# Mamba prologue: which weights the first group of loads holds, and when the convolution's diagonals are made

## What is computed

```python
xz = einsum('bld,ed->ble', hidden_states, in_proj_w)        # hidden_states: layer norm of x, 16 x 512 x 256
x, z = xz[..., :d_inner], xz[..., d_inner:]                 # d_inner = 512
xc = depthwise_conv(x, conv_w, width 4, causal) + conv_b
u = xc * sigmoid(xc)
x_dbl = einsum('bld,ed->ble', u, x_proj_w)                  # dt_lo, B_ssm, C_ssm
delta = softplus(dt_lo @ dt_proj_w.T + dt_proj_b)
A = -exp(A_log)
h = exp(delta * A) * h + (delta * u) * B_t                  # over the 512 steps
y = (h . C_t) + u * D_param
out = (y * silu(z)) @ out_proj_w.T
```

## Time and profile before

| | us |
|---|---|
| median of 3 runs | 3397.47 |
| lowest and highest of them | 3393.35, 3407.66 |
| the profiled execution | 3421.41 |
| its span in the profile | 3419.6 |

### The profile page before, as it was taken

One profiled execution on the slowest core, in us unless ns is written; L12 is line 12 of the kernel. 1 busy time (PEld: TensorE's weight loads), 2 busy tenths in 40 slices (PEclk: granted clock), 3 DMA queues, 4 the chain that ended last, 5 costly groups with the idle time before them and its releaser, 6 DMA issues.

```text
span 3419.6 us, 54089 instructions
## 1 busy us (share of the span) xinstructions
PE 2720.6 (80%) x20202; PEld 1499.2 (44%) x20202; DVE 2304.3 (67%) x2483; ACT 1717.5 (50%) x3115; POOL 2152.2 (63%) x1317
## 2 busy tenths in 40 slices
PE   5778778887788877888652699977888888359998
PEld 2333333343334433343332455555665666235665
DVE  1799999999999999999985322115556555542211
ACT  3677777777777777777640222223333433122222
POOL 1899999999999999999970344433333333024542
PEclk9899999988899998999775799989999999679999
DMA  3456555666556665565522133330111111213432
GB/s 110 106 134 154 142 136 128 146 147 147 131 135 139 149 143 137 139 141 131 142 63 59 40 78 82 88 60 26 39 51 39 45 39 39 65 31 82 87 88 25
DMA packets 227391, 330.01 MB, mean 97 GB/s; under 512 B 40545, under 2 KB 116833, under 8 KB 227010
## 3 DMA queue, kind: packets, MB, share of 16 engines
q1 hardware_dynamic: 202562, 292.49, 34.5%
q0 software_dynamic: 24576, 34.10, 5.9%
HBM read 240.52 MB, written 85.98 MB: 95 GB/s over the span
## 4 chain that ended last, share of the span: by engine, by line
PE 41%; DVE 24%; POOL 21%; issue 8%; ACT 3%; DMA 1%; another core or an unknown queue 1%; SPq 0%; DVEq 0%; POOLq 0%; ACTq 0%
POOL m_side L584 13%; DVE m_pair L668 8%; POOL m_hc L593 7%; PE f_h L1341 7%; PE g_h L1341 6%; PE t_wb L2056 6%; DVE m_hc L668 5%; PE f_yp L1355 3%; PE m_wk L771 3%; PE g_yp L1355 3%; DVE m_hc L677 2%; PE t_num L2056 2%; PE m_y L863 2%; PE m_pair L919 2%; PE t_a_ps L2056 2%
## 5 line engine op out<-in xcount | busy, mean ns | idle before, releaser
L584 POOL TENSOR_TENSOR m_side<-m_du_r,m_bc 128x1024 f32<-128x1024 f32 x416 | 974.8, 2367 | 13.6 <-DMA m_du_r<-ddd 13.3
L351 ACT ACTIVATE m_pair<-m_delta_r,m_a_neg 128x512 f32<-128x512 f32 x832 | 539.7, 681 | 179.3 <-DVE m_hc L677 128.8
L593 POOL TENSOR_TENSOR m_hc<-m_hc,m_bc 128x1024 f32<-128x1024 f32 x208 | 492.2, 2369 | 96.5 <-DVE m_hc L668 94.7
L668 DVE TENSOR_TENSOR_SCAN m_pair<-m_pair,m_side 128x1024 f32<-128x1024 f32 x240 | 548.0, 2284 | 3.3 <-ACT m_pair L351 2.8
L863 PE MATMUL m_y<-m_hc,m_fold 128*32 128x512 f32 x2048 | 321.6, 702 | 229.8 <-DVE m_hc L677 121.1
L668 DVE TENSOR_TENSOR_SCAN m_hc<-m_pair,m_side 128x1024 f32<-128x1024 f32 x176 | 397.9, 2276 | 25.9 <-ACT m_pair L351 25.9
L677 DVE TENSOR_TENSOR m_hc<-m_pair,m_bc 128x1024 f32<-128x1024 f32 x304 | 370.7, 1219 | 7.3
L771 PE MATMUL m_wk<-m_xnT,m_w_in 128*128 128x512 f32 x512 | 273.9, 662 | 11.2 <-DVE m_cw_diag L725 10.3
L771 PE MATMUL m_wk<-m_xs,m_cw_diag 128*128 128x512 f32 x512 | 246.1, 609 | 15.5 <-ACT m_xs L416 15.5
L919 PE MATMUL m_pair<-m_b_diag,m_du_t 128*32 128x128 f32 x6144 | 203.7, 289 | 43.6 <-DVE m_hc L668 24.4
L919 PEld LDWEIGHTS m_pair<-m_b_diag,m_du_t 128*32 128x32 f32 x6144 | 178.8, 117 | 124.9 <-issue 123.5
(11 more groups left out here) (308 smaller groups left out, 4929.9 us busy)
## 6 DMA issues: line engine op xcount, KB each, us to landing
m_delta_r<-ddd SPq DMA_DIRECT2D x256, 256.0 KB, 6.8
m_du_r<-ddd SPq DMA_DIRECT2D x256, 256.0 KB, 7.7
m_bc<-bcd SPq DMA_DIRECT2D x256, 128.0 KB, 2.9
ddd<-m_delta SPq DMA_DIRECT2D x32, 512.0 KB, 3.5
ddd<-m_du SPq DMA_DIRECT2D x32, 512.0 KB, 4.2
f_w<-in_w SPq DMA_DIRECT2D x24, 512.0 KB
g_w<-in_w SPq DMA_DIRECT2D x24, 512.0 KB
m_xt<-in_x SPq DMA_DIRECT2D x16, 512.0 KB, 10.8
```

The costliest lines, as they stand in the source:

```text
L351: last = nc.scalar.activation(to, delta_r[:, c % 2, q, :], ACT.Exp, scale=a_neg[:, c * NQ + q, st:st + 1])
L584: nc.gpsimd.tensor_tensor(side[:, un % RING, :, :], du_r[:, c % 2, 2 * h:2 * h + 2, :], bc[:, 0, st:st + 1, :].to_broadcast([P, 2, T]), AL ...
L593: nc.gpsimd.tensor_tensor(hc[:, un % RING, :, :], hc[:, un % RING, :, :], bc[:, 1, st:st + 1, :].to_broadcast([P, 2, T]), ALU.mult).then_i ...
L668: nc.vector.tensor_tensor_scan(to, decay, added, 0.0, ALU.mult, ALU.add).then_inc(S["scan"], 1)
```

## The change

Four things. `m_conv_w` and `m_conv_b` are counted with the first group of loads (they are still issued third and fourth of the weights, at the same place in SP's order). DVE waits for the first group and makes the convolution's diagonals first, raising `diag` once for each channel tile; only then does it wait for the second group, make `m_d_diag` (with a new semaphore `ddiag`) and negate `m_a_neg`. PE no longer waits for `diag` ahead of `ix`, but for `dt + 1` of it ahead of each `conv`, and waits for `ddiag` ahead of `xp`. ACT waits for the first group ahead of its loop over `dt`, and takes the exponential of `A_log` behind the second `cv_out`, with the wait for the second group there.

```diff
-        first_loads = [(ident, w["ident"]), (w_in, w["in_T"])]
-        loads = [(conv_w, w["conv_w"]), (conv_b, w["conv_b"]), (a_log, w["a_rep"]),
-                 (w_x, w["x_T"]), (w_dt, w["dt_T"]), (d_par, w["d_par"]),
+        first_loads = [(ident, w["ident"]), (w_in, w["in_T"]), (conv_w, w["conv_w"]), (conv_b, w["conv_b"])]
+        loads = [(a_log, w["a_rep"]), (w_x, w["x_T"]), (w_dt, w["dt_T"]), (d_par, w["d_par"]),
                  (w_out, w["out_T"]), (w_g, w["g_P"]), (fold, w["fold"])]
...
-                act.wait_ge(S["ld_w"], 16 * len(loads))
-                nc.scalar.activation(a_neg[:], a_log[:], ACT.Exp).then_inc(S["a_exp"], 1)
+                act.wait_ge(S["ld_w0"], 16 * len(first_loads))
                 for dt in range(KD):
                     ix_out(0, dt)
                     cv_out(0, 0, dt)
+                    if dt == 1:
+                        act.wait_ge(S["ld_w"], 16 * len(loads))
+                        nc.scalar.activation(a_neg[:], a_log[:], ACT.Exp).then_inc(S["a_exp"], 1)
...
-                dve.wait_ge(S["ld_w"], 16 * len(loads))
-                dve.wait_ge(S["a_exp"], 1)
-                nc.vector.tensor_scalar(a_neg[:], a_neg[:], LEAST, -1.0, ALU.max, ALU.mult).then_inc(S["aneg"], 1)
                 dve.wait_ge(S["ld_w0"], 16 * len(first_loads))
-                for k in range(KD):
-                    nc.vector.tensor_scalar(d_diag[:, k, :], ident[:], d_par[:, k:k + 1], None, ALU.mult)
                 for k in range(KD):
                     for i in range(CW):
                         last = nc.vector.tensor_scalar(cw_diag[:, k, i, :], ident[:], conv_w[:, k, i:i + 1], None,
                                                        ALU.mult)
-                last.then_inc(S["diag"], 1)
+                    last.then_inc(S["diag"], 1)
+                dve.wait_ge(S["ld_w"], 16 * len(loads))
+                for k in range(KD):
+                    last = nc.vector.tensor_scalar(d_diag[:, k, :], ident[:], d_par[:, k:k + 1], None, ALU.mult)
+                last.then_inc(S["ddiag"], 1)
+                dve.wait_ge(S["a_exp"], 1)
+                nc.vector.tensor_scalar(a_neg[:], a_neg[:], LEAST, -1.0, ALU.max, ALU.mult).then_inc(S["aneg"], 1)
...
-                pe.wait_ge(S["diag"], 1)
                 for dt in range(KD):
                     ix(0, dt)
+                    wait_alone(pe, S["diag"], dt + 1, S["tick"])
                     conv(0, dt, 0)
                     conv(0, dt, 1)
                 pe.wait_ge(S["ld_w"], 16 * len(loads))
                 pe.wait_ge(S["one"], 1)
+                pe.wait_ge(S["ddiag"], 1)
```

More of the change, by code:

```diff
@@ L183, in mamba @@
         wk = s.ps("wk", [P, 2, T])
-        first_loads = [(ident, w["ident"]), (w_in, w["in_T"])]
-        loads = [(conv_w, w["conv_w"]), (conv_b, w["conv_b"]), (a_log, w["a_rep"]),
-                 (w_x, w["x_T"]), (w_dt, w["dt_T"]), (d_par, w["d_par"]),
+        first_loads = [(ident, w["ident"]), (w_in, w["in_T"]), (conv_w, w["conv_w"]), (conv_b, w["conv_b"])]
+        loads = [(a_log, w["a_rep"]), (w_x, w["x_T"]), (w_dt, w["dt_T"]), (d_par, w["d_par"]),
                  (w_out, w["out_T"]), (w_g, w["g_P"]), (fold, w["fold"])]
         names = ("tick ld_w0 ld_w ld_x ld_xr st_x1 st_xn1 st_sc st_bc ld_bc0 ld_bc1 ld_bc2 ld_bc3 st_dd0 st_dd1 ld_r0 ld_r1 ld_r2 ld_r3 "
-                 "a_exp aneg const one halo diag "
+                 "a_exp aneg const one halo diag ddiag "
                  "bs agg ve rstd nm xn tr trev ix ixev cv cvev u iz izev sz xp xdev dt "
```

## The result

| | us | runs |
|---|---|---|
| before, median | 3401.94 | 21 |
| changed kernel, median | 3392.75 | 21 |
| ratio, with its 95% interval | 0.9976 (0.9969 to 0.9983) | |

The change saves 9.2 us by the medians and 8.2 us (5.8 to 10.5) by the ratio. The forecast was 9.6 us less, and the time 3387.9 in a range of 3377 to 3400. The median lies 4.9 above 3387.9; 4.5 of that is the kernel before, whose median was 3397.47 over three runs and is 3401.94 over 21.

A forecast was written before the change was run, and what follows sets the result against it. The prediction took the prologue's wait for the last weight (`m_fold`, landed at 19.06) as the bound: 9.6 + 0 + 0 − 0 = 9.6 us, so 3397.47 − 9.6 = 3387.9 us, range 3377 to 3400.

The forecast's parts named there:

- The wait that goes: PE's first projection waits only for `m_xnT` and starts at 14.07 instead of 23.66 us: gain 9.6 us.
- When the first group lands: Loads ahead of transposes and diagonals: landing taken as 10.3 us, between 9.8 and 19.06; costs 0 up to 11.30.
- The diagonals, the exponential, the added waits at cost 0: DVE's diagonals, ACT's exponential near 31 us and the new waits on DVE and PE are all covered: cost 0.
- The clock, a term of 0: TensorE's clock in the first channel tile and `xp`: same loss as before, 0; ends +5.5 and −6.1 us.
- The path: From the first projection the prologue is one PE-ACT chain to POOL's first scan input, which comes near 81 us.
- Rival A: TensorE's clock in the prologue comes back too: 5.5 us more gain, 3382.4 us; chance 0.12.
- Rival B: The first group's small loads land late, after 11.30 us: worst case gain 2.0 us, 3395.5 us; chance 0.06.
- Rival C: Something that doesn't move, a transfer above all, sets the first scan: no gain, 3397.5 us; chance 0.04.
- Rival D: TensorE's clock in the attention falls to 0.90, costing about 44 us: slower, 3431.9 us; chance 0.06.
- Carrying microseconds over: The prologue runs once, so the 9.6 us come off the median of the runs as microseconds, not as a share.

The follow-up runs named there:

- e1: The changed kernel without an edit, run once more as reference: 3390.21 us, ratio 0.9967 to the kernel before.
- e2: The changed kernel, but PE waits for all four channel tiles of diagonals ahead of its first projection: 3393.52 us, ratio 0.9972.
- e3: The changed kernel, but ACT takes the exponential, with its wait for the last weight, ahead of its loop again: 3393.33 us, ratio 0.9973.
- e5: The changed kernel, but PE's transposes wait for the last weight as well: 3398.08 us, ratio 0.9992.
- e7: The changed kernel with seven filler products of a zeroed tile on PE ahead of the first transpose: 3390.78 us, ratio 0.9977.
- e10: The changed kernel with filler products at four places on PE and half the `b_diag` tiles left to batch 0's first scan steps: 3396.86 us, ratio 0.9949.
- e12: The kernel before, unchanged, run once more: 3412.8 us, ratio 0.9994.
- e8: The changed kernel with PE fillers: seven ahead of the first transpose, four ahead of `xp`, eleven ahead of batch 1's transposes: 3389.87 us, ratio 0.9973.
- e4: The changed kernel, but the convolution's weights count with the second group again, and DVE and ACT wait for it: 3393.45 us, ratio 0.9974.
- e11: The kernel before, with the load of `m_w_dt` (97 partitions) cut into 96 and 1: 3407.26 us, ratio 0.9985.
- e6: The changed kernel with fills of six unread tiles on DVE delaying the layer norm, some 21 us of work: 3408.06 us, ratio 1.0025.

## Why the prediction was right

- **The wait that goes.** Right in place and size. Predicted start of the first projection 14.07, measured 14.10 in `e1` and `e2`; gain of this term 9.56, against 9.6.
- **When the first group lands.** I took 10.3; DVE starts on the diagonals at 9.49 in `e1`, and at 7.9 to 9.1 in `e2`, `e3`, `e5` and `e7` to `e10`. The lower end of 9.8, "`m_w_in`'s landing", was no bound: that transfer took 8.0 us in the profile of before, 6.5 in `e12` and between 5.4 and 5.8 in all others. It cost nothing, as a landing up to 11.30 is covered. The landing at 11.8, estimated with the fixed 2 us of the Trainium skill ("DMA: Bandwidth & Descriptors", Anatomy of one DMA, which gives it for transfers that GpSimd issues, while these are SP's), didn't come. `m_conv_b` landed 0.8 (`e8`) to 2.2 us (`e1`) behind `m_w_in`, so in `e1` the 2 us are about right, but `m_w_in` itself was there earlier.
- **The diagonals, the exponential, the added waits at cost 0.** Right. The exponential runs at 28.78 (not near 31, since the first channel tile was 2.2 us shorter), and delays nothing: the next copy starts 1.72 us after the start of the `cv_out` before it, as in the tiles beside it. The gap between a projection and its convolution is still 0.68 in all but the first tile. `e2`, `e3` and `e4` show besides that none of the three parts that they take back is worth more than about 1.4 us of waiting once the others are in, which the prediction had not said.
- **The clock, a term of 0.** The reason given beside it holds: the moment at which the clock rises isn't tied to the program (the rule of the Trainium skill, "TensorE: Matmul & The Clock Gate", Part 1; `e12` agrees, 7.97 against 10.03 us). That the term came out near 0 is luck. What I had missed are two more places, `dtp` and `iz`; the latter takes from 7.22 to 10.20 us. Between `before` and `e1` the first scan moved by 9.56 (first projection) + 2.22 (first channel tile) − 1.00 (`xp` and `dtp`) − 2.50 (`iz`) = 8.28 us, and for `e2` by 5.76.
- **The path.** Right up to POOL's input, but that input isn't what the first scan waits for. It waits for ACT in both kernels, whose work behind `iz` (9.44 us of `b_diag` tiles and more) the prediction doesn't name. The shift passes through it all the same.
- **Rival A** (all comes back) didn't happen by itself; `e10` shows its price when it is brought about. **Rival B**: `e5` gives its worst case at 21.72, as worked out, but the first group isn't late. **Rival C** (hidden anyway) falls by the table of scans (beyond some 3 us). **Rival D** (slower in the attention) isn't seen: the granted clock between 2400 and 2900 us is 0.98 in `e1`, where the last of the earlier trace rows has 0.99:

```profile
2400.00:2900.00 500.00, 435.14 (x4469) 311.38 (x4468) 292.36 (x477) 190.00 (x375) 179.60 (x182) 0.98 0.13 42
```

- **Carrying microseconds over.** Right: 8.2 (5.8 to 10.5) measured, 9.6 forecast.

## What to carry to other kernels

Where several loads count on one semaphore, ask for each waiter which of them it reads; the wait for the rest is pure loss, but only as long as nothing else covers it, so look for what is late next and stop where the parts are covered. Before a late load is worked around, look at why it is late: here one tile of 97 partitions held back all behind it. In a stretch that runs once, compare a landmark at its end (the first scan), not spans, which the later stages blur by more than such a change is worth.

## What the runs showed of the hardware

**A load of 97 partitions.** The first row is the transfer rate in the profile of before, in 40 slices from 12 to 20 us. The tail at 18 to 26 GB/s begins near 17.4 us; before it other transfers run beside it, so that the mean between 14 and 19 us is 130, not some 20 as the expectation of `e11` has it. In the second row, 17 to 19 us, the last two numbers are the mean busy share of the 16 transfer engines and GB/s: 0.07 is about one engine of sixteen (0.0625).

```profile
GB/s 98 169 164 143 232 312 379 364 287 271 169 72 87 143 205 230 215 205 379 353 348 220 189 149 47 31 41 20 20 20 23 18 26 20 26 26 26 20 26 26
...
17.00:19.00 2.00, 0.00 (x0) 0.00 (x0) 0.00 (x0) 0.00 (x0) 0.00 (x0) 1.00 0.07 25
```

With `m_w_dt` in 96 + 1 rows that tail is gone (`e11`). The Trainium skill ("DMA: Bandwidth & Descriptors", Why a DMA increments its semaphore by 16 and not by 1) says that a transfer uses the greatest number of engines, up to 16, that divides its outer size: worked out from that, one for 97 partitions and sixteen for 96. The 0.07 of the row and the missing tail in `e11` agree.

**The clock falls without a long wait.** I had looked for falls only in PE's long idle gaps, like the 4.20 us ahead of `xp`. In `e1` it fell once more between two halves of `dtp`, where PE was idle for 1.88 us (53.10 to 54.98), and in `e7` after 2.13 us. Busy time by stretch; the third number from the end is the granted clock:

```profile
54.00:55.00 1.00, 0.02 (x1) 0.02 (x1) 0.69 (x1) 0.97 (x3) 0.00 (x0) 0.90 0.71 225
55.00:56.00 1.00, 1.00 (x2) 0.48 (x2) 0.00 (x0) 0.97 (x2) 0.00 (x0) 0.50 0.87 246
56.00:60.00 4.00, 3.07 (x5) 0.71 (x4) 1.38 (x2) 2.82 (x6) 2.45 (x2) 0.50 1.05 238
60.00:68.00 8.00, 8.00 (x13) 3.30 (x14) 2.39 (x9) 2.12 (x5) 4.16 (x6) 0.68 1.02 322
```

The 0.90 of the first row places the fall at about 54.8, inside the gap, and the low level (0.50, 1.2 GHz) then lasted to about 65, in the middle of `iz`. In the profile of before PE has the same 1.88 us gap at the same place, and the clock stayed at 1.00. The four profiles without a second fall and without fillers (before, `e4`, `e6`, `e11`) are those in which `xp` took 5.09 to 5.25 us; in all others without fillers ahead of it it took 5.34. Why is open. One filler behind the second `dtp` went with an `iz` of 7.23 us in `e10`; `e4` and `e6` have 7.22 and 7.23 without it, so one run doesn't show that the filler did it.

**The clock column at the start.** It reads 1.00 from the start of a profile to the first recorded change, also where products run at the low level: in the profile of before it has 1.00 between 23 and 26 us, where PE makes the products of the earlier trace rows that take up to 1192 ns. There the durations tell the level, not the column.
